# Destination rows merged on TensorE for the last 70 of 125 chunks, in a graph attention kernel

## The chip, the cores and the metric

The kernel runs on one core of a Trainium2 chip. The metric is device time in microseconds (us) of one execution. Engines: TensorE (PE), VectorE (DVE), ScalarE (ACT), GpSimd (POOL), SyncE (SP, which issues DMAs only). DMAs issued by SP and ACT have their descriptors made by hardware; the indirect gathers, one row per partition by an index held in SBUF, are issued by POOL.

## The reference

Two layers over a graph of 12,500 nodes (64 numbers each) and 400,000 edges sorted by destination. Cut to what is computed:

```python
h_proj = einsum('nd,rde->rne', x, relation_weight)           # 32 relations
att    = sum(h_proj[etype, src] * tanh(h_proj[etype, dst] + efeat), -1)
a      = segment_softmax(att, dst)
h_nb   = segment_sum(x[src] * a[:, None], dst)
x1     = layernorm(x + leaky((x + h_nb) @ w1.T) + leaky((x * h_nb) @ w2.T))
rst    = segment_sum((x1 / out_deg)[src], dst) / in_deg
out    = layernorm(x1 + rst)
```

So each edge needs three rows: the projection of its source, the source itself, and the projection of its destination. As the edges are sorted by destination, the destinations of an edge list walk through the nodes once, from first to last.

## The kernel before, in words

**Layout.** The 400,000 edges lie as 128 partitions x 3125, partition p holding a consecutive run. A chunk is 25 edges of every partition, so there are 125 chunks. All is fp32 but the one-hots of the histogram, which are bf16.

**Stage 1, the table (lines 603 to 784).** For each of 98 blocks of 128 nodes, TensorE multiplies x by the 32 relation matrices (L726), DVE and ACT copy the result out of PSUM (L738), and SP stores it (`store`, L669 to 674) as rows of the DRAM tensor `table`. A node has 4 rows of 9 vectors: four projections, x itself, four projections. A source gather takes 5 neighbouring vectors (1280 bytes), in which x and the wanted projection both are. Four row buffers stand between copies and stores.

**Stage 2, attention over edges (from L787 on).** POOL issues, for each of the 25 edges of a chunk, one gather `gs` (L881) and one gather `gd` (L884, the destination's projection, 256 bytes). Two buffers each; the gathers of chunk c + 2 start once DVE has worked out its indices (`edge_rows`, L585 to 602) at the end of chunk c. DVE's order in a chunk is written out: `front` makes one-hots of source and destination numbers for the histogram of the next chunk (`hots`, L917) and the mask of equal neighbours; `back` waits for `gd`, adds it to the edge features (L945), waits for tanh from ACT, multiplies with the five vectors (L953, L955), reduces (L960, L961), picks one of the results by three bits of the relation (L963 to L970), runs the running maximum (L972), waits for the exponentials from ACT, and runs the segmented sums as two scans (L986). ACT copies edge features to PSUM (`take`, L1067), does tanh and exp, and stores the running sums (`sums0`). TensorE only takes the histogram, 25 matmuls per chunk (L1115). One operand of each large DVE operation lies in PSUM: the tanh argument `arg`, the weights, the comparison row of the one-hots.

**Later stages.** `attention_nodes` (98 gathers at L171, seven masks at L188), a second pass over the edges with one gather per edge column (L1157), `mean_nodes` (98 gathers at L65, 14 masks at L458).

**What sets the order.** Each engine has its own program, in loops over pairs of chunks; semaphores tie them. Nothing is planned at run time.

## Time and profile before

| what | value |
|---|---|
| median of 3 runs | 13879.36 us (13875.66 to 13880.18) |
| span of the profiled execution, first to last instruction | 12369.8 us |
| busy PE, DVE, ACT, POOL | 1185.1, 6601.1, 2202.0, 9098.1 us |
| mean granted TensorE clock | 0.544 of full speed |
| moved by DMA | 1168.46 MB |
| gathers in stage 2 / second pass | 6250 / 3125 |

The profile gives the span of the profiled execution; the times of the runs are whole executions, and what lies around the span is not in it. Busy time leaves out register, branch, semaphore and DMA-issuing instructions, except POOL's indirect gathers, which count as POOL's busy time. A share of busy time is a mean over stages with different limits, so the stretches are to be read one by one.

### The profile page before, as it was taken

Reading aid. Unit: us, or ns where it says so; the run is one execution under the profiler, and the core shown is the slowest. Engines: PE = TensorE matmul, PEld = TensorE weight load, DVE = VectorE, ACT = ScalarE, POOL = GpSimd, SP = SyncE. Lnnn points to the kernel's source line nnn. Section 1 sums busy time; section 2 is a strip of 40 time slices with the busy share of each in tenths; the row PEclk is TensorE's granted clock in tenths of the full one; section 3 lists DMA queues with packets and bytes.
Section 4 is the critical chain, followed back from the end, with each engine's and each line's share of the span. In section 5 each row is a group of like instructions: output and inputs, shape, how many; then the busy total and the mean of one; then the engine's idle time right before and its main releaser. Section 6 shows DMA issues by size and latency. Waiting matters only on the chain. (4 is left out here: it accounts for less than half of the span.)

```text
span 12369.8 us, 38117 instructions
## 1 busy us (share of the span) xinstructions
PE 1185.1 (10%) x4902; PEld 615.2 (5%) x4902; DVE 6601.1 (53%) x6162; ACT 2202.0 (18%) x1913; POOL 9098.1 (74%) x9774
## 2 busy tenths in 40 slices
PE   7110001111111111111111110030000000000001
PEld 2000000000000000000000000030000000000001
DVE  5677777777777777777777777761111111111113
ACT  5111111111111111111111111132222222222221
POOL 1777777777777777777777777757777777777777
PEclk9555555555555555555555555555555555555555
DMA  9433333333333333333333333322222212222222
GB/s 388 122 106 106 106 105 106 106 103 103 105 106 106 106 106 105 106 106 106 105 106 106 106 106 106 103 59 53 53 53 53 53 50 53 53 53 53 53 53 51
DMA packets 457192, 1168.46 MB, mean 94 GB/s; under 512 B 189459, under 2 KB 192819, under 8 KB 444099
## 3 DMA queue, kind: packets, MB, share of 16 engines
q0 software_dynamic: 356304, 723.97, 23.7%
q1 hardware_dynamic: 63490, 235.98, 5.1%
q10 hardware_dynamic: 37376, 208.28, 4.4%
q8 instruction: 7, 0.11, 0.0%
q14 instruction: 15, 0.12, 0.0%
HBM read 837.51 MB, written 330.02 MB: 94 GB/s over the span
## 5 line engine op out<-in xcount | busy, mean ns | idle before, releaser
L1157 POOL DMA_INDIRECT gy<-ytab,idx x3125 | 2948.5, 944 | 1011.6 <-issue 952.0
L881 POOL DMA_INDIRECT gs<-table,idx_s x3125 | 2954.4, 945 | 962.5 <-issue 962.5
L884 POOL DMA_INDIRECT gd<-table,idx_d x3125 | 2949.1, 944 | 951.5 <-issue 951.5
L1192 DVE TENSOR_TENSOR_SCAN run<-keep,add 128x1664 f32<-128x1664 f32 (+1 forms) x126 | 453.2, 3597 | 3013.8 <-ACT add L1222 3013.8
L1115 PE MATMUL banks<-hi,lo 128*128 128x392 bf16 x3125 | 805.2, 437 | 6932.8 <-DVE hi L917 6932.8
L917 DVE TENSOR_TENSOR hi<-banks,digit 128x9800 bf16<-128x9800 f32 x125 | 1294.5, 10356 | 0.0
L945 DVE TENSOR_TENSOR banks<-banks,gd 128x1600 f32<-128x1600 f32 (+1 forms) x126 | 229.3, 1820 | 1780.7 <-DMA gd<-table,idx_d 1780.7
L1222 ACT COPY add<-gy 128x1600 f32<-128x1600 f32 (+1 forms) x126 | 400.8, 3181 | 2351.0 <-DMA gy<-ytab,idx 2351.0
L1073 ACT ACTIVATE banks<-banks 128x1600 f32<-128x1600 f32 (+1 forms) x126 | 186.3, 1478 | 3375.6 <-DVE banks L945 3375.1
L1115 PEld LDWEIGHTS banks<-hi,lo 128*128 128x128 bf16 x3125 | 382.3, 126 | 7355.7 <-DVE hi L917 6981.7
L955 DVE TENSOR_TENSOR gs<-banks,gs 128x4800 f32<-128x4800 f32 (+1 forms) x126 | 643.7, 5108 | 0.0
L961 DVE TENSOR_REDUCE att_of<-gs 128x75 f32<-128x4800 f32 (+1 forms) x126 | 643.2, 5104 | 0.0
L1085 ACT COPY rowbuf<-run 128x1625 f32<-128x1625 f32 (+1 forms) x126 | 410.5, 3258 | 978.0 <-DVE run L986 978.0
L953 DVE TENSOR_TENSOR prod<-banks,gs 128x3200 f32<-128x3200 f32 (+1 forms) x126 | 436.7, 3466 | 204.5 <-ACT banks L1073 204.5
L1226 ACT COPY rowbuf<-run 128x1600 f32<-128x1600 f32 (+1 forms) x126 | 399.9, 3174 | 476.8 <-DVE run L1192 476.8
L986 DVE TENSOR_TENSOR_SCAN run<-banks,add 128x858 f32<-128x858 f32 (+1 forms) x252 | 466.0, 1891 | 4.4
L1075 ACT ACTIVATE banks<-ex_in 128x25 f32<-128x25 f32 (+1 forms) x126 | 24.5, 195 | 2417.6 <-DVE ex_in L975 2417.6
L917 DVE TENSOR_TENSOR lo<-banks,digit 128x3200 bf16<-128x3200 f32 x125 | 436.5, 3492 | 10.5 <-PE banks L1115 6.2
L960 DVE TENSOR_REDUCE att_of<-prod 128x50 f32<-128x3200 f32 (+1 forms) x126 | 436.2, 3462 | 4.3
L523 PE MATMUL ps_cm<-tail,mask_m 128*128 128x64 f32 x196 | 43.6, 423 | 4004.8 <-DVE mask_m L458 4004.8
L981 DVE TENSOR_TENSOR add<-gs,banks 128x1600 f32<-128x1600 f32 (+1 forms) x126 | 395.0, 3135 | 4.4
L523 PEld LDWEIGHTS ps_cm<-tail,mask_m 128*128 128x128 f32 x196 | 42.3, 331 | 4006.1 <-DVE mask_m L458 4006.1
(196 smaller groups left out, 3071.1 us busy)
## 6 DMA issues: line engine op xcount, KB each, us to landing
table<-rows SPq DMA_DIRECT2D x98, 1152.0 KB, 7.4
sums<-rowbuf ACTq DMA_DIRECT2D x124, 825.0 KB, 3.7
ef<-in_edge_attr_dram SPq DMA_DIRECT2D x125, 800.0 KB, 5.2
sums<-rowbuf ACTq DMA_DIRECT2D x124, 800.0 KB, 3.4
gs<-table,idx_s POOLq DMA_INDIRECT x3125, 2.9
gd<-table,idx_d POOLq DMA_INDIRECT x3125, 2.4
gy<-ytab,idx POOLq DMA_INDIRECT x3125, 2.4
out_dram<-y_m SPq DMA_DIRECT2D x13, 224.0 KB, 2.6
```

The costliest lines, as they stand in the source:

```text
L881: pool.indirect_dma_start(out=gs[:, s, g, :], out_offset=None, in_=table_vec, in_offset=bass.IndirectOffsetOnAxis(ap=idx_s[:, s, g:g + 1], ...
L884: pool.indirect_dma_start(out=gd[:, s, g, :], out_offset=None, in_=table_vec, in_offset=bass.IndirectOffsetOnAxis(ap=idx_d[:, s, g:g + 1], ...
L917: last = nc.vector.tensor_tensor(hot[:, :, :], iota_ps[:, 0:width].unsqueeze(1).to_broadcast([P, 2 * G, width]), digit[:, k, :, :].rearran ...
L953: nc.vector.tensor_tensor(prod[:, t0:t1, :, :], arg_t.unsqueeze(2).to_broadcast([P, n, 2, D]), vec[:, :, 0:5:4, :], ALU.mult)
L955: nc.vector.tensor_tensor(vec[:, :, 1:4, :], arg_t.unsqueeze(2).to_broadcast([P, n, 3, D]), vec[:, :, 1:4, :], ALU.mult).then_inc(ef_free, 1)
L960: nc.vector.tensor_reduce(att_of[:, 0:5:4, t0:t1].rearrange("p c g -> p g c"), prod[:, t0:t1, :, :], AX.X, ALU.add)
L961: link.then(nc.vector.tensor_reduce(att_of[:, 1:4, t0:t1].rearrange("p c g -> p g c"), vec[:, :, 1:4, :], AX.X, ALU.add))
L986: last = nc.vector.tensor_tensor_scan(run_t[:, w0:w1, :].rearrange("p w t -> p (w t)"), keep[:, 0:(w1 - w0) * (1 + n)], add_t[:, w0:w1, :] ...
L1085: nc.scalar.copy(rowbuf[:, s, t0:t1, 0:W], run_t[:, :, 1:].rearrange("p w t -> p t w"))
L1115: last = nc.tensor.matmul(hist, lo[:, 2 * g:2 * g + 2, :].rearrange("p e l -> p (e l)"), hi[:, 2 * g:2 * g + 2, :].rearrange("p e h -> p ( ...
L1157: pool.indirect_dma_start(out=gy[:, s, g, :], out_offset=None, in_=ytab, in_offset=bass.IndirectOffsetOnAxis(ap=idx[:, s, g:g + 1], axis=0 ...
L1192: nc.vector.tensor_tensor_scan(run_t.rearrange("p w t -> p (w t)"), keep_t.rearrange("p w t -> p (w t)"), add_t.rearrange("p w t -> p (w t)"),
```

## The change

The destination projection of an edge is gathered as before in the first 55 chunks (`FAR`). For the last 70 chunks it is no longer gathered. Instead TensorE works it out during the first 55 chunks. The edges of those 70 chunks form 1792 tiles of 125 edges (`MT`). The table is read in windows of 4 nodes: 128 projections (4 nodes x 32 relations), one per partition. A step multiplies a one-hot of 128 x 125 (which of the window's projections each edge of the tile wants) with a window of 128 x 64, and adds to the tile's place in PSUM. Tiles and windows both go upwards, so that a merge of the two lists takes at most 4916 steps: each step moves on by a tile or by a window. A block is 15 steps (`K`), 6 blocks per chunk (`PER`), 330 blocks. At the end of a block the tile that goes on is carried over from the block before by a matmul with the identity. ACT copies the 1024 columns out, SP stores them to `proj_d`, and in the last 70 chunks SP loads 25 columns of edges per chunk from there, in pieces of 256 bytes.

Which tile and window each step takes is worked out in stage 1 from the destinations: one-hots and a prefix sum on TensorE, lists written to DRAM and read back (`pe_tab` for TensorE's registers, `sp_tab` for SP's), and 39 gathers of tile keys. The source's two bits of selection go with a new table layout: 16 rows per node of three vectors (projection, x, projection), of which a source gather takes two (512 bytes).

```diff
+TPP = (CHUNKS - FAR) // 5; TILES = P * TPP; K = 15; PER = 6; BLOCKS = PER * FAR
-        table = nc.dram_tensor("table", (NPAD * R // 8, 9 * D), F32).ap()
+        table = nc.dram_tensor("table", ((NPAD + 4 * 3) * PAIR_ROWS, VECS * D), F32).ap()
...
+                    def picks(c, j):
+                        b, k = PER * c + j, j % 2
+                        dve.wait_ge(key_in[k], 16 * (PER // 2 * c + j // 2 + 1))
+                        if j >= 2 or later(c):
+                            dve.wait_ge(found_mm, b - 1)
+                        nc.vector.tensor_scalar(pick[:, k, :], keyb[:, k, :], lane[:, 0:1], None,
+                                                ALU.is_equal).then_inc(pick_ready, 1)
...
+                    def walk(c, j):
+                        b, k = PER * c + j, j % 2
+                        _, slots = nc.values_load_multi_w_load_instructions(
+                            pe_tab[0:1, bass.ds(16 * b, 16)], engines=[mybir.EngineType.PE], min_val=0, max_val=K,
+                            skip_runtime_bounds_check_because=MADE)
+                        if j >= 2 or later(c):
+                            pe.wait_ge(found_ready, b - 1)
+                        for h in range(2):
+                            nc.tensor.matmul(acc[k][:, h * BANK:(h + 1) * BANK], zero[:, 0:P], zero[:, :], start=True, stop=False)
+                        pe.wait_ge(win_in[k], 32 * (PER // 2 * c + j // 2 + 1))
+                        pe.wait_ge(pick_ready, b + 1)
+                        for t in range(K):
+                            at_w = nc.s_assert_within(slots[0] - slots[t] + t, 0, K - 1, skip_runtime_bounds_check_because=MADE) if t else 0
+                            nc.tensor.matmul(acc[k][0:MT, bass.ds(slots[t] * D, D)], pick[:, k, t * MT:(t + 1) * MT],
+                                             win[:, k, bass.ds(at_w, 1), :].rearrange("p o d -> p (o d)"), start=False, stop=False)
+                        nc.tensor.matmul(acc[k][:, BANK:BANK + D], zero[:, 0:P], zero[:, 0:D], start=False, stop=True)
+                        if j or later(c):
+                            pe.wait_ge(found_ready, b)
+                        nc.tensor.matmul(acc[k][:, 0:D], ident[:, :], found[:, 1 - k, bass.ds(slots[K] * D, D)],
+                                         start=False, stop=True).then_inc(found_mm, 1)
...
+                    def take_found(b, k):                      # ACT
+                        act.wait_ge(found_mm, b + 1)
+                        if later(b) and later(b - 1):
+                            act.wait_ge(found_out, 16 * (b - 1))
+                        nc.scalar.copy(found[:, k, :], acc[k]).then_inc(found_ready, 1)
...
+                    def inputs(b, k):                          # SP
+                        g0 = nc.values_load(sp_tab[0:1, bass.ds(2 * b, 1)], ...)
+                        if later(b) and later(b - 1):
+                            sp.wait_ge(found_mm, b - 1)
+                        for h in range(2):
+                            sp.dma_start(win[64 * h:64 * h + 64, k, :, :],
+                                         windows[:, bass.ds(g0, K), 2 * h * D:(2 * h + 1) * D]).then_inc(win_in[k], 16)
+                        sp.dma_start(keyb[:, k, :],
+                                     step_list[bass.ds((b * K + 1) * MT, K * MT)].unsqueeze(0).to_broadcast([P, K * MT])).then_inc(key_in[k], 16)
+                    def outputs(b, k):
+                        i0 = nc.values_load(sp_tab[0:1, bass.ds(2 * b + 1, 1)], ...)
+                        sp.wait_ge(found_ready, b + 1)
+                        if later(b):
+                            sp.wait_ge(found_out, 16 * b)
+                        sp.dma_start(proj_d[:, bass.ds(i0, K + 1), :],
+                                     found[:, k, :].rearrange("p (i d) -> p i d", d=D)).then_inc(found_out, 16)
+                    def projected(c, s, k, c5):
+                        sp.wait_ge(slot_ready, c + 1)
+                        sp.dma_start(gd[:, s, :, :], proj_v[:, bass.ds(k, 1), G * c5:G * c5 + G, :].rearrange("p o e d -> p (o e) d")).then_inc(pd_in[s], 16)
```

In a far chunk DVE's order is: pick 0, `hots` of the next chunk, pick 1, wait for `gd`, addition, pick 2, wait for tanh, two products and two reductions, pick 3, the short operations, the masked copy, pick 4, the weighted rows and the scans, pick 5, `edge_rows`. ACT copies block 5 of the chunk before and block 0 ahead of tanh, block 1 behind it, block 2 behind the exponentials, blocks 3 and 4 behind the store of the sums. TensorE does the chunk's histogram and then walks 0 to 5. SP does `inputs` of a block, then `outputs` of the block two before.

The work on the edges themselves changes with it:

```diff
-                        nc.vector.tensor_tensor(arg_t, arg_t, gd[:, s, t0:t1, :], ALU.add).then_inc(tanh_arg, 1)
+                        nc.vector.tensor_tensor(arg_t, arg_t, ef[:, s, t0:t1, :], ALU.add).then_inc(tanh_arg, 1)   # arg_t is now gd, in SBUF
...
-                        nc.vector.tensor_tensor(prod[:, t0:t1, :, :], arg_t.unsqueeze(2).to_broadcast([P, n, 2, D]),
-                                                vec[:, :, 0:5:4, :], ALU.mult)
-                        nc.vector.tensor_tensor(vec[:, :, 1:4, :], arg_t.unsqueeze(2).to_broadcast([P, n, 3, D]),
-                                                vec[:, :, 1:4, :], ALU.mult).then_inc(ef_free, 1)
+                        nc.vector.tensor_tensor(prod[:, t0:t1, :], arg_t, vec[:, :, 0, :], ALU.mult)
+                        link.then(nc.vector.tensor_tensor(arg_t, arg_t, vec[:, :, 1, :], ALU.mult))
```

Two reductions of 1600 elements stand in place of those of 3200 and 4800; one selection by the relation's lowest bit in place of three; ACT no longer copies the edge features. The histogram's one-hots are 128 and 98 wide in place of 64 and 196, in 50 matmuls per chunk in place of 25. The indices are loaded whole in stage 1. Stage 1 stores rows of 12,288 bytes per partition and block in place of 9216.

## Rows read from the trace of the kernel before

**Rows 1.** The page's head: span, busy time and share by engine, POOL in 40 slices.
```profile
span 12369.8 us, 38117 instructions
...
PE 1185.1 (10%) x4902; PEld 615.2 (5%) x4902; DVE 6601.1 (53%) x6162; ACT 2202.0 (18%) x1913; POOL 9098.1 (74%) x9774
...
POOL 1777777777777777777777777757777777777777
```
**Rows 2.** The page's groups: the three indirect gathers; busy us, mean ns | idle before.
```profile
L1157 POOL DMA_INDIRECT gy<-ytab,idx x3125 | 2948.5, 944 | 1011.6 <-issue 952.0
L881 POOL DMA_INDIRECT gs<-table,idx_s x3125 | 2954.4, 945 | 962.5 <-issue 962.5
L884 POOL DMA_INDIRECT gd<-table,idx_d x3125 | 2949.1, 944 | 951.5 <-issue 951.5
```
**Rows 3.** Busy time by stretch (windows); last three columns clock, DMA share, GB/s.
```profile
0.00:306.00 306.00, 223.44 (x882) 84.36 (x882) 153.15 (x323) 155.59 (x393) 54.68 (x203) 0.97 0.97 390
306.00:8135.00 7829.00, 807.78 (x3135) 383.94 (x3135) 5715.27 (x4923) 951.78 (x884) 5903.43 (x6250) 0.55 0.37 106
8135.00:8320.00 185.00, 110.28 (x689) 104.60 (x689) 133.07 (x229) 92.75 (x228) 95.61 (x98) 0.50 0.28 53
8320.00:12230.00 3910.00, 0.00 (x0) 0.00 (x0) 512.77 (x503) 990.22 (x380) 2948.51 (x3125) 0.50 0.20 52
12230.00:12370.00 140.00, 43.65 (x196) 42.33 (x196) 86.89 (x185) 11.66 (x28) 95.88 (x98) 0.50 0.23 47
...
160.00:300.00 140.00, 106.06 (x430) 39.91 (x428) 75.00 (x166) 75.47 (x191) 25.66 (x94) 1.00 0.99 409
```
**Rows 4.** Waits of 2000 to 7000 us: us in total, times, longest.
```profile
DVE banks L945 <- DMA gd<-table,idx_d: 1143.0, 80, 15.1
```
**Rows 5.** Groups of 2000 to 7000 us, shapes apart.
```profile
L917 DVE TENSOR_TENSOR hi<-banks,digit 128x9800 bf16<-128x9800 f32 x80 | 828.5, 10356 | 0.0
L955 DVE TENSOR_TENSOR gs<-banks,gs 128x4800 f32<-128x4800 f32 x81 | 417.0, 5148 | 0.0
L961 DVE TENSOR_REDUCE att_of<-gs 128x75 f32<-128x4800 f32 x80 | 411.5, 5144 | 0.0
L953 DVE TENSOR_TENSOR prod<-banks,gs 128x3200 f32<-128x3200 f32 x81 | 282.9, 3492 | 131.7 <-ACT banks L1073 131.7
L917 DVE TENSOR_TENSOR lo<-banks,digit 128x3200 bf16<-128x3200 f32 x80 | 279.3, 3492 | 2.8
...
L1115 PEld LDWEIGHTS banks<-hi,lo 128*128 128x128 bf16 x2000 | 246.1, 127 | 4750.8 <-DVE hi L917 4508.2 <-issue 188.4
...
L945 DVE TENSOR_TENSOR banks<-banks,gd 128x1600 f32<-128x1600 f32 x80 | 146.6, 1833 | 1143.0 <-DMA gd<-table,idx_d 1143.0
```
**Rows 6.** DVE in order of time, two rows of the chunk at 4059 us.
```profile
4059.44 3.49 DVE L953 TENSOR_TENSOR prod<-banks,gs 128x3200 f32<-128x3200 f32 x1 [1.62 <-ACT banks L1073]
...
4089.73 0.18 DVE L910 TENSOR_SCALAR digit<-src_sb 128x25 int32 x1 [0.41 <-issue]
```
**Rows 7.** By line, ns min/median/max (gathers and masks); then one pair in order of time.
```profile
L881 POOL DMA_INDIRECT gs<-table,idx_s x3125: 942/946/992, 307.1 to 8111.9; - x196
...
L171 POOL DMA_INDIRECT landed_n<-sums,node_end x98: 940/944/1837, 8135.7 to 8260.0; - x98
...
L188 DVE TENSOR_SCALAR mask_n<-iota_row,shifted_n x7: 1148/1148/1154, 8135.9 to 8142.3; 128x1792 f32<-128x1792 f32 x7
...
L458 DVE TENSOR_SCALAR mask_m<-iota_row,shifted_m x14: 676/686/687, 12231.9 to 12349.6; 128x896 f32<-128x896 f32 x14
...
12258.92 1.25 POOL L65 DMA_INDIRECT rows_m<-sums,idx_m  x1 [0.30 <-issue]
```
**Rows 8.** Sequences of matmuls in order of time; a semaphore instruction of SP, min/median/max ns.
```profile
4040.77 7.13 PE L1115 MATMUL banks<-hi,lo 128*128 128x392 bf16 x25 [54.45 <-DVE hi L917]
...
8167.61 3.25 PE L383 MATMUL ps_o<-wT,bothT 64*128 64x64 f32 x28
...
12259.19 6.24 PE L523 MATMUL ps_cm<-tail,mask_m 128*128 128x64 f32 x28 [20.28 <-DVE mask_m L458]
...
L671 SPq EVENT_SEMAPHORE  x196: 27/28/28, 11.0 to 297.4; - x196
```

More of the change, by code:

```diff
@@ L7 @@
 I32 = mybir.dt.int32
+U8 = mybir.dt.uint8
 ALU = mybir.AluOpType
@@ L29 @@
 SLOPE = 0.01
+PAIR_ROWS = R // 2
+VECS = 3
+KEYS = 4 * R
+MT = 5 * G
+FAR = 55
+TPP = (CHUNKS - FAR) // 5
+TILES = P * TPP
+WINDOWS = NPAD // 4
+STEPS = TILES - 1 + N // 4
+K = 15
+PER = 6
+BLOCKS = PER * FAR
+UC = -(-(BLOCKS * K + 1) // P)
+SPARE_W = K
+MADE = "made by the program itself, in these bounds"
 assert T * P == E and NB * P >= N and G * CHUNKS == T and GB * GROUPS == NB and GROUPS % 2 == 0
+assert KEYS == P and BLOCKS * K >= STEPS and FAR % 5 == 0 and FAR % 2 == 1 and PER % 2 == 0
 def later(count):
@@ L599, in edge_rows @@
[L599 to L602 removed]
+            link.then(nc.vector.tensor_scalar(half[:, :], type_sb[:, at], 1, None, ALU.logical_shift_right))
@@ L673, in store @@
                                      rows[:, s:s + 1, :, :].rearrange("p o r c -> p o (r c)")).then_inc(stored[s], 16)
-                    each_block(sp, store, False)
+                    opening(sp, store, False)
+                    sp.dma_start(src_sb[:, 0:T], src_v).then_inc(idx_in, 16)
+                    with nc.allow_non_contiguous_dma(reason="one number of each partition"):
+                        sp.dma_start(head_next[0:P - 1, :], dst[T:E].rearrange("(p t) -> p t", p=P - 1)[:, 0:1]).then_inc(idx_in, 16)
@@ new lines, in _ @@
+                    part(sp, store, 6, 12)
+                    sp.wait_ge(cum_ready, 1)
+                    with nc.allow_non_contiguous_dma(reason="a list by step from one by partition"):
+                        sp.dma_start(cum_list[16:].rearrange("(c p) -> p c", p=P), cum_i[:, :]).then_inc(cum_out, 16)
+                    part(sp, store, 12, 14)
+                    sp.wait_ge(cum_out, 48)
+                    for v, at in enumerate((16, 17, 1)):
+                        sp.dma_start(cum_at[:, v, :, :],
+                                     cum_list[at:at + BLOCKS * K].rearrange("(p b j) -> p b j", b=LB, j=K)).then_inc(cum_in, 16)
@@ L875, in _, with gather @@
+                    for m in range(10):
+                        near(0, m)
+                    with sp.Fori(1, (CHUNKS - FAR) // 10) as n:
+                        for m in range(10):
+                            near(n, m)
                 @block.gpsimd
                 def _(pool):
-                    def gather(c, s, early=G):
+                    def gather(c, s, both, early=G):
                         pool.wait_ge(slot_ready, c + 1)
@@ L891, in _ @@
-                    gather(CHUNKS - 1, 0, early=EARLY)
+                            if both:
+                                pool.indirect_dma_start(
+                                    out=gd[:, s, g, :], out_offset=None, in_=table_vec,
+                                    in_offset=bass.IndirectOffsetOnAxis(ap=idx_d[:, s, g:g + 1], axis=0)).then_inc(gd_in[s], 16)
+                    with pool.Fori(0, FAR // 2) as i:
+                        gather(2 * i, 0, True)
+                        gather(2 * i + 1, 1, True)
@@ L928, in front @@
+                    def front(c, link, far=False):
+                        if far:
+                            picks(c, 0)
+                        if not (isinstance(c, int) and c == CHUNKS - 1):
+                            hots(c + 1, link)
+                        if far:
+                            picks(c, 1)
                         at = bass.ds(c * G, G)
                         at_d = bass.ds(c * G + 1, G)
-                        if not (isinstance(c, int) and c == CHUNKS - 1):
-                            hots(c + 1)
@@ L947, in back @@
+                        nc.vector.tensor_tensor(arg_t, arg_t, ef[:, s, t0:t1, :], ALU.add).then_inc(tanh_arg, 1)
+                        if far:
+                            picks(c, 2)
                         if t0:
@@ L1119, in _ @@
+                    histogram(0)
+                    for j in range(PER):
+                        walk(0, j)
+                    with pe.Fori(1, FAR) as c:
+                        histogram(c)
+                        for j in range(PER):
+                            walk(c, j)
+                    with pe.Fori(FAR, CHUNKS) as c:
+                        histogram(c)
+                    nc.tensor.matmul(hist, zero[:, 0:P], zero[:, 0:2 * NB], start=False, stop=True).then_inc(hist_done, 1)
                     pe.wait_ge(counted, 1)
```

535 lines of the change are left out of this document (354 added, 181 removed).

## The prediction

> **What bounds the kernel now.** I read the page's head first, then the stretches, then one steady chunk. The head shows GpSimd (POOL) busy for 74% of a span of 12369.8 us and level from the second slice on [rows 1]. Its three large groups are indirect gathers of equal price: 945, 944 and 944 ns each, whether a row holds 1280 or 256 bytes, with 0.30 to 0.32 us of "issue" before each [rows 2]. That is 1.25 us per gather, and no wait stands in it. The stretches put 306 us on building the table, 7829 on the attention edges, 185 on the nodes, 3910 on the second pass and 140 on its nodes [rows 3]. In the attention stretch 125 chunks of 50 gathers make 7804 us, 62.4 us per chunk. VectorE (DVE) waits there for the gathered rows, 1143.0 us in 80 chunks or 14.3 us in each [rows 4], so its own path is 62.4 - 14.3 = 48.1 us long. POOL is the bound, DVE the next.
>
> **Own time.** The sum is made against the span of the profiled execution. The median shown, 13879.4 us, is 1509.6 us longer. Nothing in the trace shows what that is made of; I take it as fixed.
>
> **The attention stretch, near half (the last 70 chunks).** 25 destination gathers per chunk go, so POOL needs 25 x 1.25 = 31.2 us. DVE's path of 48.1 us shrinks too: the one-hots go from 13,000 to 11,300 elements at 1.04 ns (10356 and 3492 ns for 9800 and 3200) [rows 5], -1.8 us; the products from 8.6 us (3492 + 5148 ns) to two of 1600 elements, 3.7 us at the price of the 1600-element addition (1833 ns) [rows 5], -5.0; the reductions by the same, -5.0; some eight short operations of 0.1 to 0.3 us go, -1.3. That leaves 35.0 us, in which the wait for tanh (1.62 us) [rows 6] stays, for nothing else is queued there. 35.0 is above 31.2: what is late next is DVE, and it paces the near half, 70 x 35.0 = 2450 us. The 3200 pieces of 256 bytes that SP now loads for a chunk have a chunk's time to land: the second pass moves as many, and writes 0.82 MB, in a chunk at a DMA share of 0.20 [rows 3]. No gain and no loss there, except that the first such load stands behind the last walk and its store on SP: some 15 us, once.
>
> **Far half (the first 55 chunks).** POOL keeps its 50 gathers, 62.4 us. Beside them come, per chunk, six windows, six one-hot builds ("picks") on DVE, six walks on TensorE, six copies of 1024 columns on ScalarE and six stores.
>
> DVE: a pick reads 1875 bytes in SBUF and writes SBUF. The nearest rows are the masks, one SBUF source and a scalar from SBUF: 1148 ns for 1792 elements, 686 for 896 [rows 7], half the price per element of the row with PSUM. By them a pick is 1.2 us, six are 7.2, and DVE's path is 42 us, hidden under 62.4. At the slow rate it would be 2.0 us each, 47 in all, also hidden.
>
> POOL beside those DVE operations: this is where hiding ends. While the masks run, gathers last up to 1837 ns instead of 944, and one that fell beside two of 0.69 us lasted 1.25 [rows 7]. Over the last nodes the extra is 95.88 - 98 x 0.944 = 3.4 us for 14 x 0.686 = 9.6 us of masks; at the first nodes 95.61 - 92.5 = 3.1 us for 7 x 1.148 = 8.0 [rows 3, 7]. So POOL loses 0.35 to 0.39 of such a DVE time; I take 0.4. Picks: 2.9 us per chunk. The change also takes the tanh argument out of PSUM, so that three 1600-element operations have both inputs in SBUF, 5.3 us. No large operation of that kind stands beside a gather before; the bounds are 0 and, each charged whole, 5.3 us. The nearest row is again the mask, which also keeps two reads of SBUF busy, so I take 0.4: 2.1 us. In the near half the same 2.1 us ends under DVE's 35.0. The far chunk is 62.4 + 2.9 + 2.1 = 67.4 us.
>
> The Trainium skill ("SBUF — State Buffer", SBUF: two separate sides) calls the port pair that VectorE shares with GpSimd a lock held for a whole instruction, taken by two-port modes and, against a GpSimd operation that reads SBUF, by operations with two SBUF inputs. The stretched gathers agree with the first half, and no row shows the second. By that rule in full the far chunk would go to 74.9 us; it is a rival below.
>
> TensorE: a walk is 16 fp32 matmuls of 64 columns at 6.24 / 28 = 0.223 us with their weight loads, and two clearings of 512 columns, near 0.37 us each by the histogram (7.13 us for 25 of 392) [rows 8]: 4.4 us is its floor. Above it come 16 numbers read into registers and some 30 addresses worked out from them. The trace of before has no such read. Nearest rows: a semaphore instruction takes 0.028 us, a weight load with its matmul goes through in 3.25 / 28 = 0.116 us [rows 8], and DVE loses 0.41 us at a loop's turn, where it renews several addresses [rows 6]. From the first two, 16 x (0.12 + 8 x 0.028) = 5.5 us, clearings and waits 0.8, and 16 reads at about 0.13: w = 8.5 us per walk. Low bound 4.4; high bound, 0.41 us for each of 46 steps beside the floor, 23.
>
> For a number that only a page has: the Trainium skill ("Runtime: NRT & Kernel Launch", Instruction fetch mechanics) puts a register load at about 200 ns. By that the 16 reads take 3.2 us and w is 9.6.
>
> What w may be before it shows: the picks stand at fixed places on DVE, and each waits until the walk two before it has ended. Walks 2 to 5 follow each other, then the histogram of the next chunk (50 weight loads at 0.127 [rows 5], 6.4 us), for which DVE's one-hots (12.1 us) wait, then pick 1 (1.2) and walk 1, and only then walk 2. That ring is 5w + 20 us long. At w = 8.5 it is 62.5, hidden under 67.4; from w = 9.5 on it sets the chunk. Sum: 55 x 67.4 = 3707.
>
> The windows: from 409 GB/s at a share of 0.99 [rows 3] one DMA engine moves 25.8 GB/s. The second pass, 0.20 x 31.2 x 16 = 100 us of engine time per chunk less 32 for its write, gives 21 ns per piece of 256 bytes. 11,520 window pieces are 245 us, stores of 3.15 MB 121, keys 56; the rest goes from 369 to 247 with smaller source rows. 669 us over 16 engines is 42 of 67. A window lands in about 6 us, under w. Had hardware-queue pieces three times that price, the share would pass 1 at 70 us per chunk.
>
> Attention: 3707 + 2450 + 15 = 6172 against 7804, -1632.
>
> **The table stretch.** A block's rows go from 1152 to 1536 KB. 98 x 0.393 MB more at 409 GB/s, where DMA is full [rows 3], is +94 us. All indices are now loaded here (4.8 MB, +12). The lists are stored in 5000 pieces of 4 and as many of 125 bytes, and DVE spends 15 us on keys between blocks that have four buffers: +24 together. POOL's 39 extra gathers (49 us) stand beside stores of 3.8 us per block, hidden. +130; bounds +95 (bytes alone) and +200.
>
> **The rest** is untouched. Sum: -1632 + 130 = -1502. Span 10,868; time 13879 - 1502 = 12,377, rounded 12,380.
>
> **Rivals.**
> - *Walks pace the far half.* More sequencer work than I count: w = 11.5 gives a chunk of 77.5, +556, 12,935. For: 0.13 us per read has no row. Against: PE is busy 10% now.
> - *No loss on POOL.* Picks run at the slow rate, or gathers slip between: far chunk 62.4, -275, 12,105. For: the short SBUF operations of a chunk never lengthen a gather (942/946/992) [rows 7]. Against: the masks do.
> - *Full lock.* Every pick and two-input operation is charged whole: far 74.9, and POOL's near chunk 36.5 passes DVE's: +413 + 105, 12,900.
> - *Slower than before.* The register reads and addresses are the price: at w = 23 the ring is 135 us, +3720, 16,100. It turns the sign from 94.7 us per chunk, w = 15. For: nothing rules out a read of 0.4 us. Against: the 0.028 us row.
>
> **How the numbers follow.** Forecast 50% (own range 12,200 to 12,600), walks pace 22%, no loss 12%, full lock 8%, slower 8%. Range 12,000 to 13,150: it holds the first four with the table's bounds, and leaves out the slower one and the far ends of the walks. A change of 0.2% (28 us) is what can be told from none. Faster 0.90, the same 0.01, slower 0.09.
>
> **What would show it.** Right: far chunks of 67 us with gathers back to back and some stretched beside picks and additions; near chunks of 35 us with DVE never waiting for gathers; table stretch near 435 us; walks near 8.5 us. Wrong: POOL or DVE waiting for walks in the far half (picks that wait for TensorE), or gathers unstretched at 1.25 us. A distance between span and time other than 1510 us would make the fixed part wrong.

## The result, and the profile after

The changed kernel took 14567.99 us (median of 4 runs, 14545.81 to 14603.33), the kernel before 13877.51 beside it: a ratio of 1.0502, 95% interval 1.0483 to 1.0520. Forecast were 12,380 us, in a range of 12,000 to 13,150, with 0.90 on faster. It is slower by 690 us, and lies outside the range.

The experiments found that the kernel before has two times. On the two chips of experiments 1 to 8 it takes 13,866 to 13,890 us, on the two chips of all later ones 12,369 to 12,399, mostly 12,371. Its profile shown ahead of the prediction is of the second kind (span 12369.8), the runs shown beside it are of the first. I call them condition A (13,880) and condition B (12,370). The profile after is from condition A.

The page of the changed kernel, condition A, its head and three groups (busy, mean ns, idle before them), against [rows 1, 2]:

```profile
span 14585.8 us, 83842 instructions
PE 3723.8 (26%) x19430; PEld 3152.0 (22%) x19596; DVE 5361.0 (37%) x5501; ACT 2358.4 (16%) x2118; POOL 7990.0 (55%) x8066
...
L1109 POOL DMA_INDIRECT gs<-table,idx_s x3125 | 3118.7, 998 | 4471.9 <-DVE idx_d L618 3020.1
L1455 POOL DMA_INDIRECT gy<-ytab,idx x3125 | 3230.5, 1034 | 1176.9 <-issue 1117.0
L1153 DVE TENSOR_TENSOR lo<-banks,digit 128x6400 bf16<-128x6400 f32 x125 | 853.1, 6825 | 3587.4 <-PE banks L1382 3217.5
```

POOL is no longer level: 3020.1 us of waiting for VectorE's indices stand before its gathers, where [rows 2] had none. VectorE in turn has waited 3217.5 us for TensorE's histogram (L1382) before it could build the next one-hots. The stretches, against [rows 3] (table, far half, near half, nodes, second pass):

```profile
0.00:466.00 466.00, 256.64 (x901) 94.66 (x902) 191.44 (x348) 162.06 (x393) 130.68 (x245) 0.82 0.95 358
466.00:6890.00 6424.00, 2879.12 (x13657) 2532.34 (x13815) 2103.59 (x2029) 645.57 (x636) 2634.09 (x2750) 0.50 0.37 97
6890.00:9830.00 2940.00, 430.70 (x3988) 375.39 (x3994) 2338.97 (x2208) 456.51 (x453) 1804.89 (x1750) 0.53 0.39 104
9830.00:10043.00 213.00, 113.66 (x689) 107.31 (x689) 132.84 (x228) 92.47 (x228) 95.75 (x98) 0.50 0.23 46
10043.00:14391.00 4348.00, 0.00 (x0) 0.00 (x0) 504.14 (x503) 985.09 (x375) 3230.11 (x3125) 0.50 0.19 47
```

Far gathers run from 466.2 to 6888.6, 116.8 us per chunk (forecast 67.4). The last source gather starts at 9764.3, 41.1 per near chunk (35.0). The second pass, which the change does not touch, takes 4348 us against 3910 on the page of before: that alone says the two pages are not of one condition.

One far chunk of the timeline (start, us, what, idle before). TensorE:

```profile
3152.52 0.66 PE L1404 MATMUL banks<-found,ident 128*128 x2
3154.25 1.32 PE L1382 MATMUL banks<-hi,lo 128*128 128x98 bf16 x14 [1.07 <-issue]
3158.11 0.24 PE L1382 MATMUL banks<-hi,lo 128*128 128x98 bf16 x1 [2.54 <-issue]
...
3196.67 0.24 PE L1382 MATMUL banks<-hi,lo 128*128 128x98 bf16 x1 [2.56 <-issue]
3199.47 0.24 PE L1382 MATMUL banks<-hi,lo 128*128 128x98 bf16 x1 [2.56 <-issue]
3202.28 0.24 PE L1382 MATMUL banks<-hi,lo 128*128 128x98 bf16 x1 [2.57 <-issue]
3205.94 0.24 PE L1382 MATMUL banks<-hi,lo 128*128 128x98 bf16 x1 [3.42 <-issue]
3207.34 1.55 PE L1382 MATMUL banks<-hi,lo 128*128 128x98 bf16 x17 [1.16 <-issue]
```

and POOL, ScalarE and SP's queue in the same stretch:

```profile
3136.86 0.95 POOL L1109 DMA_INDIRECT gs<-table,idx_s  x1 [56.20 <-DVE idx_d L618]
...
3198.55 0.94 POOL L1113 DMA_INDIRECT gd<-table,idx_d  x1 [0.30 <-issue]
3200.96 1.01 ACT L1320 COPY found<-banks 128x1024 f32<-128x1024 f32 x1 [60.72 <-issue]
3202.23 4.38 SPq L1048 DMA_DIRECT2D win<-table  x2
```

POOL's burst of 50 gathers runs without a break from 3136.86 to 3199.5. Fourteen matmuls of the histogram go at once, then they come one every 1.4 to 3.7 us with no wait between them that the code has, and the last 17 run together from 7.8 us after the end of the burst. ScalarE's next copy, whose walk had ended at 3153.2, and SP's next loads also start only 1.5 and 2.7 us after the burst. I call this the crawl. VectorE waits 60.5 us for this histogram. Only then can it work through its chunk, at the end of which the next indices stand, and POOL is idle for 56.3 us. Burst (62.6 us) and the rest of the chunk (56.3 us) thus lie one behind the other: 118.9 us here.

### The profile page after: what moved, and what is told of

Same layout as the page of the kernel before. It is cut to its first block and busy times, and to the rows that moved or that the text cites. A ratio compares the mean times of both kernels' runs of the same rounds, so it can differ in the third digit from the quotient of the medians.

```text
span 14585.8 us, 83842 instructions
## 1 busy us (share of the span) xinstructions
PE 3723.8 (26%) x19430; PEld 3152.0 (22%) x19596; DVE 5361.0 (37%) x5501; ACT 2358.4 (16%) x2118; POOL 7990.0 (55%) x8066
## 5 line engine op out<-in xcount | busy, mean ns | idle before, releaser
L1109 POOL DMA_INDIRECT gs<-table,idx_s x3125 | 3118.7, 998 | 4471.9 <-DVE idx_d L618 3020.1
L1455 POOL DMA_INDIRECT gy<-ytab,idx x3125 | 3230.5, 1034 | 1176.9 <-issue 1117.0
L1399 PEld LDWEIGHTS banks<-win,pick 128*125 128x125 f32 x9900 | 2156.4, 331 | 307.0 <-issue 281.2
L1153 DVE TENSOR_TENSOR lo<-banks,digit 128x6400 bf16<-128x6400 f32 x125 | 853.1, 6825 | 3587.4 <-PE banks L1382 3217.5
L1399 PE MATMUL banks<-win,pick 128*125 (+1 forms) x9900 | 2132.2, 413 | 150.4 <-issue 114.9
L1382 PE MATMUL banks<-hi,lo 128*128 128x98 bf16 x6250 | 769.9, 271 | 4950.8 <-issue 2865.1
L1382 PEld LDWEIGHTS banks<-hi,lo 128*128 128x128 bf16 x6250 | 533.6, 133 | 5184.2 <-issue 3076.1
L1113 POOL DMA_INDIRECT gd<-table,idx_d x1375 | 1320.3, 960 | 419.2 <-issue 419.2
L1320 ACT COPY found<-banks 128x1024 f32<-128x1024 f32 x330 | 333.7, 1011 | 4685.7 <-remote 2247.2
L1167 DVE TENSOR_SCALAR pick<-keyb,lane 128x1875 f32<-128x1875 uint8 x330 | 396.2, 1201 | 1085.1 <-DMA keyb<-step_keys 876.6
L1153 DVE TENSOR_TENSOR hi<-banks,digit 128x4900 bf16<-128x4900 f32 x125 | 656.4, 5251 | 0.0
L1394 PE MATMUL banks<-zero 128*128 128x512 bf16 x495 | 274.7, 624 | 705.3 <-issue 631.1
```

The costliest lines, as they stand in the source:

```text
L1109: pool.indirect_dma_start(out=gs[:, s, g, :], out_offset=None, in_=table_vec, in_offset=bass.IndirectOffsetOnAxis(ap=idx_s[:, s, g:g + 1], ...
L1113: pool.indirect_dma_start(out=gd[:, s, g, :], out_offset=None, in_=table_vec, in_offset=bass.IndirectOffsetOnAxis(ap=idx_d[:, s, g:g + 1], ...
L1153: last = nc.vector.tensor_tensor(hot[:, :, :], iota_ps[:, 0:width].unsqueeze(1).to_broadcast([P, 2 * G, width]), digit[:, k, :, :].rearran ...
L1167: nc.vector.tensor_scalar(pick[:, k, :], keyb[:, k, :], lane[:, 0:1], None, ALU.is_equal).then_inc(pick_ready, 1)
L1382: last = nc.tensor.matmul(hist[:, e * NB:(e + 1) * NB], lo[:, 2 * g + e, :], hi[:, 2 * g + e, :], start=False, stop=False)
L1399: nc.tensor.matmul(acc[k][0:MT, bass.ds(slots[t] * D, D)], pick[:, k, t * MT:(t + 1) * MT], win[:, k, bass.ds(at_w, 1), :].rearrange("p o ...
```

## Experiments

Theory S: during an unbroken burst the other engines get on slowly, whatever they do. Rivals named one suspect each. Runs 1 to 8 are in condition A (1 to 4 on chip 1, 5 to 8 on chip 8), the others in B (chip 2, the last repeats of 9 and 12 on chip 7).

**1. The kernel before, again** (no edit). 

> The kernel before, unchanged, for a trace of its own. Its profiled execution had a span of 12370 us where the runs took 13878; the changed kernel's span and time agree within 2 us. Theory A (the page of before shows an execution in which gathers were cheaper): the span here is near 13,870 us and gathers or their issue are stretched. Theory B (1500 us lie around the span): span near 12,370 again.


Measured 13871.47 us, ratio 0.9998 (0.9987 to 1.0009), profiled span 13881.2. Its stretches, against [rows 3]:

```profile
0.00:306.00 306.00, 222.14 (x882) 83.64 (x882) 153.49 (x325) 155.99 (x393) 55.12 (x203) 0.97 0.96 390
306.00:9036.00 8730.00, 802.72 (x3127) 380.61 (x3127) 5639.33 (x4819) 936.75 (x862) 6582.64 (x6250) 0.55 0.34 95
9036.00:9344.00 308.00, 116.31 (x697) 108.80 (x697) 203.87 (x336) 107.06 (x250) 95.83 (x98) 0.50 0.19 38
9344.00:13692.00 4348.00, 0.00 (x0) 0.00 (x0) 504.70 (x498) 985.22 (x375) 3218.63 (x3125) 0.50 0.19 47
```

The table costs the same 306 us; the attention stretch 8730 against 7829, the second pass 4348 against 3910. Its gathers average 1064, 1042 and 1030 ns where [rows 2] have 945, 944 and 944. These means mix two kinds: the medians stay at 947 to 955 ns (min/median/max below), and the extra sits in longer ones up to 1.94 us and in longer gaps before them. Only some 2 us lie around the span, as theory A has it. The 1510 us that I had put around it lie inside.

```profile
L881 POOL DMA_INDIRECT gs<-table,idx_s x3125: 945/955/1939, 306.6 to 9032.8; - x196
L1157 POOL DMA_INDIRECT gy<-ytab,idx x3125: 943/947/1937, 9344.2 to 13690.5; - x196
...
8982.96 0.33 PE L1118 MATMUL banks<-zero 128*128 128x392 bf16 x1
...
9035.34 0.25 DVE L1004 COPY moved<-banks 64x98 f32<-64x98 f32 x1 [57.96 <-remote]
```

The last two rows show that this kernel has such a stall too. VectorE's copy L1004 waits in the program for this last matmul of the histogram alone. It starts 52 us after it, with the end of the last gather (9035.25). In condition B, in the trace of the rows, the same copy starts 0.1 us after the matmul (8045.36), with gathers still going on.

**2. One loop body of 25 chunks on TensorE, in the kernel before.**
```
-with pe.Fori(0, CHUNKS) as c:
+with pe.Fori(0, CHUNKS // 25) as c25:
+    for u in range(25): ...
```


> The kernel before with TensorE's histogram written out for 25 chunks per loop turn (1250 matmuls in a body in place of 25); same work and waits. Fetch theory (while gathers are issued back to back, an engine that must take in new instructions gets them slowly; in the changed kernel TensorE's far loop body of some 760 instructions crawls at 1.4 to 2.8 us per matmul from 18 us into a burst of gathers until it ends): the 25 matmuls of a chunk take 25 x 1.4 to 2.8 = 35 to 70 us instead of 7, and the time rises by 0 to 1500 us. Rival (the walks' register reads and computed addresses hold TensorE): the histogram stays at 7 us per chunk and the time is that of before within 0.3%.


Measured 13884.35, ratio 1.0000 (0.9989 to 1.0012); 25 matmuls still pass in 5.68 us. A body of 1250 matmuls costs nothing where a chunk has 25. Since 14 to 46 pass at full pace before a crawl in the other runs, this does not rule out that instructions arrive slowly.

**3. No register reads.** Constants in place of the 16 numbers of each walk (the last 70 chunks then add the projections of other nodes).
```
-nc.tensor.matmul(acc[k][0:MT, bass.ds(slots[t] * D, D)], ..., win[:, k, bass.ds(at_w, 1), :]...
+nc.tensor.matmul(acc[k][0:MT, t * D:(t + 1) * D], ..., win[:, k, t, :]...
```


> The changed kernel with fixed places in place of the 16 numbers read per walk: no register reads on TensorE, no computed addresses; the destination rows are then the wrong ones for the last 70 chunks, all movement and matmuls stay. Fetch theory: TensorE still crawls in the histogram while gathers run, far chunk near 115 us, 14,450 to 14,600. Register rival: crawl gone, far chunk 65 to 75, about 11,800 to 12,300 by its own trace.


Measured 14445.29, ratio 1.0406 (1.0368 to 1.0444). Against the changed kernel (14567.99) the reads and addresses of 330 walks are worth 123 us, give or take some 60 by the two intervals; the crawl stays (114.4 us per far chunk).

**4. Walks in an inner loop,** a third of the code in the far loop.
```
-for j in range(PER): walk(c, j)
+with pe.Fori(0, PER // 2) as jj:
+    for j2 in range(2): walk(c, j2, jj)
```


> The changed kernel with TensorE's six walks as three turns of an inner loop over two, so that the code of a chunk is a third as long; same work and waits. Fetch theory: crawl gone or much shorter, far chunk 65 to 90 us, gain 1500 to 2800 us against the changed kernel. Register rival: no gain, within 1% of 14,568. If the crawl starts anew at each return to code that is not held, it stays.


Measured 14507.46, ratio 1.0450 (1.0420 to 1.0481), 117.0 us per far chunk. What it takes less than the changed kernel (60 us by the medians) lies in the near half, 39.7 us per chunk against 41.1. Not the cause.

**5. 235 more matmuls per chunk in the kernel before.**
```
+for u in range(235):
+    nc.tensor.matmul(hist[:, 0:D], zero[:, 0:P], zero[:, 0:D], start=False, stop=False)
```


> The kernel before with 235 more matmuls per chunk on TensorE (zeros times zeros, 128x64 bf16, added to the histogram, so nothing else changes): 260 per chunk, as many as a far chunk of the changed kernel has. They touch no DMA and no semaphore, and at the pace of a few tenths of a microsecond they fit four times over into the 63 us that TensorE waits in each chunk. Theory S (an engine gets its instructions only slowly while GpSimd issues gathers, so the count of instructions beside a burst decides): they crawl at 1 to 3 us each while gathers are issued, the histogram of the next chunk comes late, and a chunk takes 90 to 115 us instead of 70: 16,400 to 19,500 us. Theory T (SyncE's small transfers make the others wait): nothing changes, 13,850 to 13,900 us.


Measured 16310.39, ratio 1.1749 (1.1715 to 1.1783). Nothing but plain matmuls was added, and they crawl:

```profile
3134.82 0.21 PE L1119 MATMUL banks<-zero 128*128 128x64 bf16 x1 [2.59 <-issue]
3137.62 0.21 PE L1119 MATMUL banks<-zero 128*128 128x64 bf16 x1 [2.59 <-issue]
3140.42 0.21 PE L1119 MATMUL banks<-zero 128*128 128x64 bf16 x1 [2.59 <-issue]
```

Most of the slow steps are 2.80 us long, some 2.10, 1.40 or 3.50, on average 2.5; 7219.6 us of "issue" stand before these matmuls in all. Gathers from 307.0 to 11432.6 are 89.0 us per chunk. That is just under theory S's range (90 to 115 us, 16,400 and more) and far above theory T's. Neither the walks nor any new transfer is needed for the crawl. POOL's own gathers are at the price of condition B here, and POOL waits for VectorE instead:

```profile
L881 POOL DMA_INDIRECT gs<-table,idx_s x3125 | 2964.9, 949 | 4262.5 <-DVE idx_d L601 3311.8
```

**6. One step of 15 in each walk** (last 70 chunks' destination rows incomplete).
```
-for t in range(K):
+for t in range(1):
```


> The changed kernel with one of 15 steps in each walk (its last 70 chunks' destination rows are left incomplete); transfers, picks, copies and waits are all there. TensorE's matmuls of a far chunk fall from 260 records to 92. Both theories give a gain, since a walk is some 6 us shorter where it is not hidden: theory T 12,500 to 12,800 us with the histogram still crawling from about 18 us after the start of a burst until its end; theory S the crawl gone or cut to less than a third and a far chunk of 70 to 90 us instead of 118: 11,900 to 13,000 us.


Measured 14076.82, ratio 1.0140 (1.0082 to 1.0197), above both ranges. A far chunk is 108.3 us: 168 matmul records fewer save 8.5 us. The crawl starts later in the histogram (36 matmuls pass, not 14) and lasts to the end of the burst, where theory S had it gone or cut to a third. This speaks against a pure count of matmuls.

**7. No window, key and result transfers** but the first two (the last 70 chunks read rows of the table in place of the merged ones).
```
-inputs(PER * c + j, j % 2); outputs(PER * c + j - 2, j % 2)
+if not later(c) and j < 2: inputs(PER * c + j, j % 2)
...
```


> The changed kernel with SyncE's window and key loads issued for the first two blocks only and its stores of found rows left out (the destination rows of the last 70 chunks are then read from another tensor in pieces of the same size, and are wrong); all 330 walks with their 15 steps, all picks and copies stay. Theory T: no crawl, gathers and walks lie side by side, a far chunk of 63 to 75 us: 11,600 to 12,200 us. Theory S: the crawl in the histogram stays and so does nearly all of the time, 14,200 to 14,570 us.


Measured 14064.53, ratio 1.0131 (1.0074 to 1.0188), 109.8 us per far chunk, VectorE's longest wait for the histogram 65.1 us. A little below theory S's range, far from the rival's: the transfers and the waits for them are worth 503 us of the changed kernel, but they are not the cause of the crawl.

**8. Destinations gathered for all chunks,** no lists, walks, picks or window loads.
```
-with pool.Fori(FAR // 2 + 1, PAIRS) as i: gather(2 * i, 0, False) ...
+with pool.Fori(0, PAIRS) as i: gather(2 * i, 0, True) ...
```


> The changed kernel's table layout, histogram and shorter VectorE work, but destinations gathered for all 125 chunks: no lists, no walks, no picks, no window loads. Theory S: 50 matmuls per chunk instead of 25 are too few to matter, the chunk stays bound by GpSimd's 50 gathers at 62 to 70 us, 13,000 to 13,950 us. Rival (the layout itself, or the histogram of 50 smaller matmuls, brings the crawl): a chunk of 85 us or more, above 15,500 us.


Measured 15093.59, ratio 1.0872 (1.0841 to 1.0904), between the two ranges, so neither theory had it. Gathers from 405.3 to 10249.8 are 78.8 us per chunk against 69.8 of the kernel before in the same condition, though VectorE has less to do; the first 36 matmuls of a histogram of 50 pass in 3.12 us, the others crawl:

```profile
3039.86 0.24 PE L1177 MATMUL banks<-hi,lo 128*128 128x98 bf16 x1 [1.56 <-issue]
3043.35 0.24 PE L1177 MATMUL banks<-hi,lo 128*128 128x98 bf16 x1 [3.25 <-issue]
3045.45 0.24 PE L1177 MATMUL banks<-hi,lo 128*128 128x98 bf16 x1 [1.86 <-issue]
```

**9. The same with the histogram of the kernel before,** 25 matmuls of 128x392.
```
-hist[:, e * NB:(e + 1) * NB], lo[:, 2 * g + e, :], hi[:, 2 * g + e, :]
+hist, lo[:, 2 * g:2 * g + 2, :]..., hi[:, 2 * g:2 * g + 2, :]...
```


> As the kernel that gathers all 125 chunks in the new layout (15,094 us, 80.6 us per chunk), with one change: the histogram in the form of the kernel before, 25 matmuls of 128x392 per chunk instead of 50 of 128x98 (VectorE's one-hots take 1.8 us longer). Theory S (TensorE gets about one matmul's instructions per 2.8 us of a burst of gathers, so a chunk can't be shorter than its matmuls need): with 25 matmuls the supply asks for 70 us at most, a chunk of 63 to 70 us, 13,000 to 13,850 us. Rival L (the layout, its 512-byte rows or the operands in SBUF, makes the crawl): 14,900 us or more.


This and all that follow met condition B. Measured 12755.09 beside 12370.51, ratio 1.0304 (1.0287 to 1.0321). The question of condition A is not answered. In B the new table layout costs 98 us in the table stretch, and the new operands 2.3 us in each of 125 chunks (64.7 against 62.4). Two repeats (edits the same) agreed: 12744.82 (1.0303) and 12748.95 (1.0306). 

> All 125 chunks gathered in the new layout, histogram of 25 matmuls per chunk. Where the kernel before takes 12,370 us: 12,750 us again. Where it takes 13,880 us: if the number of matmuls beside a burst decides (50 of them gave 15,094 us), 13,500 to 14,300 us; if the layout does, 14,900 to 15,300 us.

 

> All 125 chunks gathered in the new layout, 25 matmuls per chunk. Where the kernel before takes 13,880 us: if the number of matmuls beside a burst decides (the same with 50 took 15,094 us), 13,500 to 14,300 us; if the layout does, 14,900 to 15,300 us. Where it takes 12,370 us: 12,740 to 12,760 us, as twice before.

**10. 25 more matmuls per chunk in the kernel before** (range(25) in the edit of 5). 

> The kernel before with 25 more matmuls per chunk (zeros times zeros, 128x64), 50 in all, where 235 more gave 16,310 us. At full pace they are 1 us of TensorE's 63 us of waiting. Theory S: the chunk goes from 70 to 75 to 85 us, 14,500 to 15,750 us. Rival L: 13,850 to 13,900 us.


Measured 12370.48, ratio 1.0000 (0.9990 to 1.0011).

**11. 60 small copies per chunk on ScalarE, in the kernel before.**
```
+for u in range(60):
+    nc.scalar.copy(junk[:, u:u + 1], ident[:, u:u + 1])
```


> The kernel before with 60 copies of 128x1 on ScalarE in each chunk, where it waits for VectorE's scans (some 8 us idle there, and 34 us more before the next chunk). Theory S in its wide form (every engine is supplied slowly beside a burst): 60 instructions at 1.4 us each or more are over 80 us, the chunk goes above 75 us and the time above 14,500 us. In its narrow form (TensorE alone): 60 copies of 0.1 to 0.2 us are hidden or nearly so, 13,850 to 14,300 us, with no gaps above 1 us between the copies.


Measured 12373.06, ratio 1.0002 (0.9991 to 1.0012); 60 copies pass in 5.67 us. In condition B nothing crawls; 10 and 11 say nothing of A, for which both were meant.

**12. Pauses between the far gathers of the changed kernel.**
```
 ... .then_inc(gd_in[s], 16)
+pool.wait_ge(pause_done, c * G + g)
+pool.memset(pause[:, :], 0.0).then_inc(pause_done, 1)
```


> The changed kernel with a fill of 128x768 zeros on GpSimd after each of the 1375 pairs of gathers of the far chunks, 0.9 to 1.3 us each by the copies of 128x384 in the table stretch (0.51 to 0.63 us); a burst goes from 62.5 to 85 to 95 us. If gathers without a break are what starves the others, the walks now run inside the burst, and a far chunk takes 88 to 100 us instead of 118: 13,000 to 13,600 us. If a break doesn't help, the pauses add to the 118: 15,800 to 16,400 us.


Measured 11831.78 beside 12370.51, ratio 0.9564 (0.9545 to 0.9583): faster than the kernel before with the pauses in it (757 ns each), at 84.2 us per far chunk. So the change itself had to be looked at in condition B. Whether a pause ends the crawl in A is not shown. Repeats: 11839.30 (0.9571) and 11839.76 (0.9571). 

> The changed kernel with a fill of 128x768 on GpSimd after each pair of far gathers. Where the kernel before takes 12,370 us: 11,830 us again. Where it takes 13,880 us: if the pauses let the others through, a far chunk of 85 to 95 us and 12,800 to 13,500 us; if they don't, the crawl stays for the whole of a burst that is now 85 us long, a far chunk of 135 to 145 us, 15,500 to 16,200 us.

 

> The changed kernel with a fill of 128x768 (0.76 us where it was measured) after each pair of far gathers, a burst of some 84 us. Where the kernel before takes 13,880 us: if a pause lets the other engines' instructions through, a far chunk of 85 to 100 us, 12,700 to 13,600 us; if not, the crawl lasts as long as the longer burst, 135 to 145 us per far chunk, 15,500 to 16,200 us. Where it takes 12,370 us: 11,830 to 11,850 us, as twice before.

**13. The changed kernel as it is, in condition B.** 

> The changed kernel as it is, beside the kernel before. If the crawl is a matter of the chip: on a chip where the kernel before takes 12,370 us, the walks run inside the bursts and a far chunk takes 62 to 72 us (the paced kernel has 84 us there, 21 us of it pauses and their waits): 10,700 to 11,400 us, a ratio of 0.86 to 0.92. If the pauses were what removed the crawl: 118 us per far chunk there too, 13,500 us or more, a ratio of 1.09. On a chip where the kernel before takes 13,880 us: 14,570 us, 1.05 again.


Measured 10915.04 (10913.98 to 10919.54) beside 12370.54, ratio 0.8825 (0.8810 to 0.8840). Its stretches:

```profile
0.00:462.00 462.00, 249.78 (x901) 92.76 (x902) 190.16 (x349) 162.30 (x393) 130.20 (x245) 0.84 0.95 362
462.00:4174.00 3712.00, 2729.51 (x13983) 2522.26 (x14145) 2161.29 (x2071) 653.05 (x649) 2874.08 (x2750) 0.52 0.65 171
4174.00:6680.00 2506.00, 322.61 (x3664) 306.91 (x3665) 2288.11 (x2178) 443.02 (x440) 1822.40 (x1751) 0.54 0.43 117
...
6863.00:10764.00 3901.00, 0.00 (x0) 0.00 (x0) 509.87 (x500) 985.19 (x375) 2948.22 (x3125) 0.50 0.21 52
```

TensorE in a far chunk there, beside gathers that never stop:

```profile
3061.41 1.03 PE L1394 MATMUL banks<-zero 128*128 128x512 bf16 x2 [5.14 <-issue]
3062.24 6.40 PE L1399 MATMUL banks<-win,pick 128*125 128x64 f32 x30
3068.43 0.26 PE L1401 MATMUL banks<-zero 128*128 128x64 bf16 x1
3068.50 0.67 PE L1404 MATMUL banks<-found,ident 128*128 x2
3068.96 3.48 PE L1382 MATMUL banks<-hi,lo 128*128 128x98 bf16 x50
```

The same 50 matmuls that took 54.6 us in condition A take 3.5. Far gathers go from 462.1 to 4173.0: 67.5 us per chunk. Time, ratio and far chunk are as expected of a matter of the chip or its condition.

**14. 235 more matmuls per chunk, in condition B.** 

> The kernel before with 235 more matmuls per chunk. Where the kernel before takes 13,880 us: 16,310 us again. Where it takes 12,370 us: if the crawl is a matter of the chip, TensorE does 260 matmuls in some 15 to 20 us of each chunk and nothing waits for it, 12,360 to 12,500 us; if bursts without a break are the cause everywhere, they crawl as before and it is 16,000 us or more.


Measured 12374.50, ratio 1.0003 (0.9993 to 1.0014), against 1.1749 in A:

```profile
3040.95 5.69 PE L1115 MATMUL banks<-hi,lo 128*128 128x392 bf16 x25 [48.81 <-DVE hi L917]
3046.47 7.02 PE L1119 MATMUL banks<-zero 128*128 128x64 bf16 x235
```

One kernel unchanged, two conditions, 30 ns per matmul or mostly 2.80 us: the crawl belongs to the condition.

## Why the prediction was wrong

**The step that failed** is the far chunk, 62.4 + 2.9 + 2.1 = 67.4 us, and in it the overlap: TensorE's walks, VectorE's picks and ScalarE's copies stand there as hidden beside the gathers. It measured 116.8 us. 55 times the difference is 2717 us, more than the whole miss of 2191 (14,568 less 12,377). (All other stretches together came out 1001 us longer than forecast, less than the 1508 us that were counted around the span and are not there.) The prediction had no term for a crawl. In the chunk shown above the histogram takes 54.6 us, VectorE waits for it, and POOL then waits 56.3 us for VectorE's indices. POOL waiting in the far half was among the prediction's own signs of being wrong, though by way of the picks and not of the histogram.

Against the kernel before in A (69.8 us per chunk) the far half loses 55 x 47.0 = 2585 us, the near half gains 70 x 28.7 = 2009, the table adds 160 and the rest gives back some 30: +705 between the spans (14585.8 - 13881.2). None of my rivals had this mechanism; "slower than before" had the right place (walks that the gathers don't hide) but another price (register reads). Experiment 3 puts that price at some 0.4 us per walk.

**A premise was wrong too**, and it hid the risk: "Own time", the 1509.6 us between span and median, "nothing in the trace shows what that is made of; I take it as fixed". Around a span lie 2 us in every run here. The 1511 us between the two spans of the kernel before are inside: 922 in the attention stretch (306.6 to 9034.2 against 307.1 to 8113.1), 447 in the second pass, 103 at the nodes between them, 41 at the last nodes. Of the first two, 949 are longer gathers and 420 longer gaps before them. The nodes' gathers are not longer (95.83 us busy against 95.61); there other engines are late, and the first gather starts 94.1 us after the last one of the edges, against 21.7. A page and a time that differ by 12% are of two conditions, and every row that I worked from was of the one in which the result was not measured.

This premise did not make the miss. Carried as a ratio of spans (0.879) the forecast would have been 12,190 us, further off. Worked out anew from the stretches of experiment 1 (chunks of 69.8 us, the other terms as forecast) it would be some 11,850, an estimate. Of the runs here only those that put work beside the gathers in condition A, such as experiment 5, show the price of the overlap.

**The steps against condition B**, the one of the rows:
- Span 10,868 forecast, 10912.2 measured; the forecast ratio of spans was 0.879, the measured one 0.882. Of the 44 us, 25 are in the table stretch and some 20 behind the last edge gather, which I had called untouched.
- Attention: 462.1 to 6636.0 is 6174, forecast 6172. Far chunk 67.5 against 67.4, near chunk 35.2 against 35.0; in the near half POOL waits for VectorE's indices, and the view of waits has no row of VectorE waiting for gathers:

```profile
POOL gs L1109 <- DVE idx_s L613: 128.2, 68, 18.7
```

- Loss on POOL beside VectorE, 5.0 us per far chunk forecast. The far gathers of condition B:

```profile
L1109 POOL DMA_INDIRECT gs<-table,idx_s x1375 | 1464.8, 1065 | 447.6 <-issue 447.6
L1113 POOL DMA_INDIRECT gd<-table,idx_d x1375 | 1409.3, 1025 | 419.1 <-issue 419.1
```

Over 0.944 that is 25 x 0.121 + 25 x 0.081 = 5.1. The part of the two-SBUF operations, forecast at 2.1, shows alone in the last repeat of experiment 9, where three of 1.82 us run between 3056.41 and 3063.5:

```profile
3057.59 1.47 POOL L966 DMA_INDIRECT gs<-table,idx_s  x1 [0.30 <-issue]
3059.36 0.94 POOL L970 DMA_INDIRECT gd<-table,idx_d  x1 [0.31 <-issue]
3060.60 1.95 POOL L966 DMA_INDIRECT gs<-table,idx_s  x1 [0.30 <-issue]
3062.86 1.43 POOL L970 DMA_INDIRECT gd<-table,idx_d  x1 [0.30 <-issue]
```

0.53 + 1.01 + 0.49 = 2.0 us for 5.5 of VectorE's, and a chunk of 64.7 us against 62.4. The Trainium skill ("SBUF — State Buffer", SBUF: two separate sides) would have each such operation hold the port for its whole length. The gathers here lose 0.37 of that length, and 5.1 us per far chunk for 12.7 us of picks and such operations. So the charge of the rival "full lock" falls; how long the port itself is held no row shows.
- A pick is 1.20 us (forecast 1.2). In condition B TensorE goes round in 67.6 us per chunk. In the chunk at 3009 us the first five walks start 7.9 to 10.2 us apart (forecast 8.5), the sixth 14.5 later, where it waits for other engines, and the next chunk's first 15.6 later, with the histogram between. The ring, forecast at 62.5, stays just hidden.
- Table stretch +155 us in B and +160 in A, forecast +130, bounds 95 to 200.

So the terms were sized well for condition B and summed for a result in condition A. A rival, "the times are of another condition than the page; what is hidden there may not be hidden here", was due a large chance.

**What stays open.** Which resource is short in condition A. Shown is that the crawl comes beside bursts of gathers, lets 14 to 46 matmuls pass first, hits plain matmuls as it hits the next steps of VectorE, ScalarE and SP, comes in multiples of 0.70 us (1.40, 2.10, 2.80, 3.50) and ends with the burst or some us behind it, up to 23 in experiment 5. It needs neither register reads nor walks nor SP's transfers. The Trainium skill ("Runtime: NRT & Kernel Launch", Instruction fetch mechanics) has instructions fetched ahead in large blocks and says that the fetch is hidden behind their issue; longer and shorter code left the chunks of its kernel as they were (experiments 2 and 4). The DMA queues of the changed kernel bear this out as far as they reach: from 900 to 6900 us in condition A, over some 50 crawling chunks, no packet of the two instruction queues moves, which over the whole run have 13 and 26:

```profile
q1 hardware_dynamic: 681440, 419.04, 25.6%
q0 software_dynamic: 81088, 124.71, 9.9%
q10 hardware_dynamic: 7200, 42.24, 1.8%
```

So the crawl is not a late load of code over these queues. That instructions get from there to the engines slowly would fit the matmuls that pass first, but no run tests it. Gathers and other engines also take turns: where TensorE crawls (experiment 5) the gathers cost 0.949 us, where it does not (experiment 1) they average 1.04 to 1.06. That both wait for one thing is a guess.

The record names the chips: 1 and 8 met condition A, 2 and 7 condition B, and no chip met both. The page of the rows (B) is older than all experiments, and those in A all came before those in B. So whether the condition is the chip's or came and went with time, I can't tell. Pauses, 25 matmuls in the new layout, and small copies all met condition B, so whether they matter in A wasn't tried.

## What to carry to other kernels

Compare the span of the page with the times before anything else: here all that lies around a span is 2 us, and a larger distance says that page and times are from two conditions. Run the kernel before again, look at which groups grew, and forecast from that page. Even that page would not have given the cost here. Work that is "hidden beside gathers" can have a price of its own: the same 235 added matmuls cost nothing on one chip and 17% on another. Adding such dummy work to the kernel before is a short experiment that shows it ahead of the change. A plan that puts hundreds of instructions beside an unbroken burst has to be timed in both conditions. In condition B this change is the best version measured (0.8825), in A the kernel before stays ahead of every variant tried.

## What the runs showed of the hardware

- Matmuls without waits beside an unbroken burst of gathers (experiments 5 and 14): mostly 2.80 us each in condition A, 0.030 in B (7.02 us for 235). From 14 to 46 of them pass at full pace first in the chunks looked at: 14 in the changed kernel, 36 in experiments 6 and 8, 25 + 21 in experiment 5.
- The same gathers of the second pass: 0.943 to 0.946 us on average in B, 1.026 to 1.034 in A in each of the nine traces there, the changed kernel's and the kernel before's alike. The median in A is 0.947 (experiment 1).
- Gathers beside VectorE's picks and operations with both inputs in SBUF, condition B: 5.1 us lost per far chunk for 12.7 us of them.
- Sixteen register reads with their addresses cost 0.37 us of the time per walk, give or take 0.18 (experiment 3), in condition A.
